# Decoder layer on one core: routing and experts in the first program, and the normaliser's magnitude and square on ScalarE

## The chip, the core and the metric

The kernel runs on one core of a Trainium2 chip. Its time is the device time of one execution in microseconds. Three executions took 796.13, 796.8 and 797.87 us, median 796.8. A profiled execution took 796.79 us. Its trace is read below; times in it count from the start of its span, which is 795.0 us long.

## The reference

A batch of 8 sequences of 256 tokens with 256 features goes through three blocks in fp32, each behind a layer norm and with a residual: gated linear attention with 16 heads; an mLSTM with 8 heads of 32; and a mixture of 8 experts, of which each token takes two.

```python
# mLSTM, per head; k_hop from a gathered table of 2017 rows
C = (qk + k_hop) * D                                  # D = exp(log_D - max_log_D)
normalizer = jnp.maximum(jnp.abs(jnp.sum(C, -1, keepdims=True)), jnp.exp(-max_log_D))
h = (C / (normalizer + 1e-6)) @ vh
hn = (h - mean(h)) / jnp.sqrt(var(h) + 1e-5)          # then weight, bias, residual
# experts
top_w, top_idx = jax.lax.top_k(logits, 2)             # then softmax over the two
for e in range(8):
    h = gelu(layernorm(x, e) @ w1[e] + b1[e]) @ w2[e] + b2[e]
    out = out + combine[..., e:e + 1] * h
```

## The kernel before

The kernel is written engine by engine: each of the five engines has its own list of instructions, and semaphores with written waits set their order. It has two programs (two `nc.Block()`), one behind the other.

The first block has three stages. The token stage (`tokens_*`) does layer norm, linear attention and the gates, batch by batch. The hop stage gathers 257 x 128 rows of the table on GpSimd's queue, turns them on TensorE, multiplies them with the queries and leaves the result in `KH`. The linear-memory stage (`mlstm_*`, lines 1104 to 1546; the mLSTM) goes over 16 units, two for each of the 8 batches. For unit `u` TensorE makes the scores (`score`), VectorE adds the hop term (`add`, lines 1429 and 1432) and multiplies with the decay (`weigh`, line 1438), for which GpSimd masks (`mask`, line 1172) and ScalarE exponentiates (`decay`, lines 1345 and 1346) a tile. TensorE multiplies with the values (`values`). The values have a column of ones, so the sum of C comes out beside h as column `DX` of the same product.

When both units of a batch are done, ScalarE copies the product from PSUM (`evict`, line 1354) and squares it (line 1358). VectorE's `spread` (lines 1440 to 1450) makes the normaliser out of column `DX` in three chained instructions on 128x16: magnitude, maximum with `EX` (with 1e-6), square times 1e-5. Then it reduces the squares to the variance (line 1448) and adds both (line 1450). The centred h needs no division by the normaliser: it scales the variance instead. ScalarE takes the inverse root (`inv_std`), VectorE multiplies (`scale`, line 1457), and GpSimd applies the weight and adds the residual (`residual`, lines 1179 and 1182). `EX` holds the exponential of the maximum; VectorE adds 1e-6 to it once (line 1500).

In the same functions, behind the last unit, stands the tail: for each batch mean and variance of the row (lines 1470 and 1477), the normalised rows (`hidden_rows`, line 1483), their turning on TensorE (line 1266), router logits (line 1277), VectorE's `add_bias` (line 1489), and a store of the rows to DRAM (`store_rows`, line 1368, the last one at line 1417) on ScalarE's queue. SyncE loads the experts' weights in `mlstm_sync` while the memory stage runs (`load_w1`, line 1098; `load_w2`, line 1101), waits for the last batch's results and clears the semaphores of the list `done_with` (`retire`). These are all that are made while `stage[0]` is `early`. The block ends at line 1547's statement, and `early.close()` frees them, so that later ones can take their numbers.

The second block is routing and experts. VectorE picks the two experts of each token and counts, TensorE makes prefix sums (lines 1868 and 1869) and, behind nine filler multiplications that the profile shows as 18 (line 1865), sorts the tokens into tiles by one-hot matrices (line 1877) that VectorE makes (`one_hot`, line 2018, and `planes`, lines 2023 to 2027). VectorE waits for the stored rows (`z_st`) ahead of `planes`, and reads the sorted result at line 2042. Then all engines loop over 39 tiles of 128 tokens: GpSimd fetches the rows (line 1831) and scatters the results with an addition (line 1851), TensorE multiplies with both weights (lines 1897 and 1906). SyncE starts this block with `prime`, 20 increments of the loop's counters, and stores the residual `X` to the output (line 1817).

## Time and profile before

| | |
|---|---|
| median of three runs | 796.8 us |
| profiled execution | 796.79 us |
| its span | 795.0 us |
| TensorE matmul busy | 731.5 us, 92% |
| VectorE busy | 408.4 us, 51% |
| ScalarE busy | 351.9 us, 44% |
| GpSimd busy | 432.1 us, 54% |
| mean granted TensorE clock | 0.974 of full speed |

The share of busy time is a mean over stages. The stages are, roughly: tokens to 200 us, hops to 355, linear memory to 444, its tail to 463, routing to 491, experts to the end. PE is TensorE, PEld its weight loads, DVE VectorE, ACT ScalarE, POOL GpSimd, SP SyncE; SPq and ACTq are their DMA queues. "L1489" is line 1489 of the kernel. `G`, `U`, `E`, `QT` and `PET` are large buffers in SBUF out of which many small tensors are cut, `ps` is PSUM.

### The profile page before, as it was taken

To read this page: it belongs to the slowest core of one execution; us is meant where nothing else is said; L and a number is where in the kernel's file an instruction comes from. 1 tells how busy PE (TensorE), PEld (TensorE's weight loads), DVE (VectorE), ACT (ScalarE), POOL (GpSimd) and SP (SyncE) were. 2 spreads that over 40 slices of the span, in tenths; PEclk is the share of its full clock that TensorE was granted. 3 is DMA by queue.
4 is the path that set the end of the run, shared out by engine and by line. 5 is a ranking of instruction groups with operands and counts; after the bars stand their busy time and mean duration, and the time that the engine had idled before them with its cause. 6 is when DMAs were issued, how large, how long until landed. Compare 5 with 4: busy or idle time off the path is not lost. (4 is left out here: it accounts for less than half of the span.)

```text
span 795.0 us, 17125 instructions
## 1 busy us (share of the span) xinstructions
PE 731.5 (92%) x5866; PEld 657.2 (83%) x5867; DVE 408.4 (51%) x982; ACT 351.9 (44%) x899; POOL 432.1 (54%) x504
## 2 busy tenths in 40 slices
PE   7899999889999999778788859999999999999992
PEld 5677777679999999777787646999999999999991
DVE  2467777756655344228999956233333333333320
ACT  1434434346665444246867411443444344434430
POOL 6567777767777777753655201244444444454432
PEclk8999999999999999899999979999999999999997
DMA  9334444432333634726777990222222122212221
GB/s 290 100 115 131 140 129 132 130 120 87 99 100 104 211 104 115 223 70 186 224 201 212 329 320 14 75 39 35 38 33 40 34 38 33 40 33 40 33 34 13
DMA packets 75813, 88.30 MB, mean 111 GB/s; under 512 B 11952, under 2 KB 66032, under 8 KB 75632
## 3 DMA queue, kind: packets, MB, share of 16 engines
q0 software_dynamic: 19824, 43.93, 22.1%
q1 hardware_dynamic: 52256, 40.12, 17.2%
q10 hardware_dynamic: 3680, 3.54, 1.3%
q8 instruction: 34, 0.56, 0.3%
q14 instruction: 19, 0.16, 0.1%
HBM read 75.83 MB, written 11.73 MB: 110 GB/s over the span
## 5 line engine op out<-in xcount | busy, mean ns | idle before, releaser
L330 POOL DMA_INDIRECT G<-in_rpe,hopi x193 | 188.6, 977 | 63.4 <-issue 53.0
L1949 ACT ACTIVATE G<-ps,U 128x128 f32<-128x128 f32 x312 | 84.7, 382 | 161.5 <-PE ps L1897 161.5
L1897 PEld LDWEIGHTS ps<-G,QT 128*128 128x128 f32 x1248 | 145.2, 192 | 1.9
L1897 PE MATMUL ps<-G,QT 128*128 128x128 f32 x1248 | 145.5, 275 | 0.0
L1906 PE MATMUL ps<-G 128*128 x624 | 142.0, 381 | 1.3 <-DVE G L2093 1.3
L1906 PEld LDWEIGHTS ps<-G 128*128 128x128 f32 x624 | 115.5, 190 | 16.3 <-issue 1.7
L1601 PE MATMUL ps<-U,PET 128*128 128x128 f32 (+3 forms) x768 | 100.3, 274 | 0.0
L1601 PEld LDWEIGHTS ps<-U,PET 128*128 128x128 f32 x768 | 94.0, 193 | 0.1
L976 DVE COPY PET<-ps 128x512 f32<-128x512 f32 x64 | 44.2, 690 | 89.3 <-PE ps L1028 87.6
L1851 POOL DMA_INDIRECT out<-G,slots x39 | 67.1, 1721 | 22.7 <-issue 22.7
L1643 ACT ACTIVATE PET<-ps 128x512 f32<-128x512 f32 (+1 forms) x63 | 37.4, 594 | 88.4 <-PE ps L1028 84.9
L1831 POOL DMA_INDIRECT G<-hidden_rows,slots x39 | 39.8, 1021 | 58.1 <-DVE U L2045 37.8
L1028 PE MATMUL ps<-cst,G 128*128 128x128 f32 x386 | 60.0, 279 | 7.3 <-DMA G<-in_rpe,hopi 7.3
L1856 POOL TENSOR_TENSOR U<-cst 128x1 f32<-128x1 f32 x39 | 7.3, 188 | 89.3 <-DMA out<-G,slots 89.3
L2063 DVE TENSOR_SCALAR G<-ps,U 128x128 f32<-128x128 f32 x78 | 28.4, 405 | 52.5 <-PE ps L1886 52.5
L1028 PEld LDWEIGHTS ps<-cst,G 128*128 128x128 f32 x386 | 46.8, 149 | 8.0 <-DMA G<-in_rpe,hopi 8.0
L675 ACT ACTIVATE U<-ps 128x512 f32<-128x512 f32 (+2 forms) x56 | 28.6, 511 | 53.1 <-PE ps L476 27.5
L1934 ACT ACTIVATE QT<-U 128x1024 f32 x39 | 43.1, 1107 | 18.5 <-DVE U L2045 18.5
L1250 PE MATMUL ps<-PET,G 128*128 128x99 f32 x256 | 41.0, 283 | 6.1 <-DVE G L1438 5.1
L330 POOL DMA_INDIRECT U<-in_rpe,hopi x38 | 37.3, 981 | 15.9 <-issue 9.1
L2051 DVE TENSOR_SCALAR QT<-U 128x1024 f32 x39 | 27.1, 695 | 35.6 <-issue 35.6
L807 DVE TENSOR_TENSOR U<-ps,cst 128x1024 f32<-128x1024 f32 x32 | 38.3, 1218 | 12.4 <-PE ps L550 8.1
(240 smaller groups left out, 1225.7 us busy)
## 6 DMA issues: line engine op xcount, KB each, us to landing
G<-run_max SPq DMA_DIRECT2D x16, 512.0 KB, 7.1
U<-in_w SPq DMA_DIRECT2D x16, 512.0 KB, 7.2
G<-in_w SPq DMA_DIRECT2D x8, 1024.0 KB, 10.3
G<-in_rpe,hopi POOLq DMA_INDIRECT x193, 2.9
U<-in_ctx SPq DMA_DIRECT2D x8, 256.0 KB, 2.8
tokens_kept<-X SPq DMA_DIRECT2D x8, 256.0 KB, 2.3
X<-tokens_kept SPq DMA_DIRECT2D x1, 2048.0 KB, 9.5
hidden_rows<-QT ACTq DMA_DIRECT2D x8, 256.0 KB, 7.3
```

The costliest lines, as they stand in the source:

```text
L330: pool.indirect_dma_start(out=dst, out_offset=None, in_=rpe_d, in_offset=bass.IndirectOffsetOnAxis(ap=hopi[:, n:n + 1], axis=0)) \
L807: nc.vector.tensor_tensor(am[n % 2], s, tri.unsqueeze(1).unsqueeze(1).to_broadcast([P, 4, 2, P]), ALU.mult).then_inc(am_r, 1)
L976: copy(PET[:, q % NPT, 0:w], bank(turn_bank(q), 512)[:, 0:w]).then_inc(pet_r[q % 2], 1)
L1028: mm = pe.transpose(o[:, n % 2, j, :], src[:, j * P:(j + 1) * P], ident)
L1250: pe.matmul(o, Dm[u % ND][:, hh, c * P:(c + 1) * P], v[0], start=True, stop=(c == 0), skip_group_check=True)
L1601: mm = pe.matmul(o, pet[:, n % 2, j, :], rhs, start=True, stop=True, skip_group_check=True)
L1831: pool.indirect_dma_start(out=z_in[u], out_offset=None, in_=z_dram, in_offset=bass.IndirectOffsetOnAxis(ap=tokg[:, u:u + 1], axis=0)) \
L1851: pool.indirect_dma_start(out=out_d, out_offset=bass.IndirectOffsetOnAxis(ap=tok[:, u:u + 1], axis=0), in_=ysb[u], in_offset=None, bounds_ ...
L1897: mm = pe.matmul(bank(1 + 2 * u + c // 4, 4, P)[:, c % 4], w1c[u][:, k, c], hT[u][:, k, :], start=(k == 0), stop=(k == KC - 1))
L1906: mm = pe.matmul(bank(7, 2, D)[:, u], gel[u][:, c, :], w2s[:, one(e), c, :].rearrange("p o n -> p (o n)"), start=(c == 0), stop=(c == NI - 1))
L1934: nc.scalar.activation(w1c[u][:, 1], w1_of(e, 1), ACT.Copy) \
L1949: ins = nc.scalar.activation(gel[u][:, c, :], bank(1 + 2 * u + c // 4, 4, P)[:, c % 4], ACT.Gelu, bias=b1c[u][:, c:c + 1])
```

## The change

Two things are changed.

One program: the second block's five functions become `experts_sync`, `experts_gpsimd`, `experts_tensor`, `experts_scalar` and `experts_vector`, made by `experts()` ahead of the one block that is left, and each engine calls its own behind its `mlstm_*`. Their bodies are as they were, but for a wait of VectorE for its own last `add_bias` at the start, a wait of SyncE for the stored rows ahead of the store of `X`, and `prime`, which moves. Only the semaphores of the token stage (33 by the code) are `early` now; `retire` clears them in `mlstm_sync`, behind the third load of second-layer weights, then `prime` and a new semaphore `fresh` follow. GpSimd waits for `fresh` ahead of its last residual, TensorE, ScalarE and VectorE in the tail.

The normaliser: ScalarE's `evict` takes the magnitude of column `DX` straight from PSUM into `nrm` ahead of its copy, and squares `nrm` behind the other square, with 1e-6 and the root of 1e-5 as bias and scale. `EX` is squared in the same way once, in place of line 1500. VectorE is left with the maximum of the two squares, which gives the same value since both are positive.

```diff
-        stage = [early]
+        stage = [late]
@@ ahead of mv_r, ..., sm_r
+        stage[0] = early
@@ behind them
+        stage[0] = late
@@ mlstm_sync
             for e in range(3):
                 sp.wait_ge(pv_full, tiles_dead(e))
                 load_w2(sp, e)
+
+            retire(sp)
+            prime(sp, counters, counters)
+            sp.sem_inc(fresh, 1)
             for e in range(NUNIT // 2 - 2, E):
...
             sp.wait_ge(lg_cp, B)
-            retire(sp)
@@ mlstm_gpsimd
             residual(B - 2)
+            pool.wait_ge(fresh, 1)
             residual(B - 1)
@@ mlstm_tensor
             logits(2)
+            pe.wait_ge(fresh, 1)
             keep_going(1)
@@ mlstm_scalar, evict
+                nc.scalar.activation(nrm[b % 2], o.rearrange("p c (h d) -> p c h d", d=NVX)[:, :, :, DX], ACT.Abs).then_inc(nrm_r, 1)
                 nc.scalar.activation(hs[b % 2].rearrange("p c h d -> p c (h d)"), o, ACT.Copy).then_inc(hs_r, 1)
                 act.wait_ge(hs_r, b + 1)
                 if b >= 1:
                     act.wait_ge(var_r, b)
-                nc.scalar.activation(sq, hs[b % 2][:, :, :, 0:DX], ACT.Square).then_inc(sq_r, 1)
+                nc.scalar.activation(sq, hs[b % 2][:, :, :, 0:DX], ACT.Square)
+                act.wait_ge(nrm_r, b + 1)
+                squared(nrm[b % 2]).then_inc(nsq_r, 1)
+
+            def squared(a):
+
+                return nc.scalar.activation(a, a, ACT.Square, scale=LN_EPS ** 0.5, bias=eps_ap[:, 2:3])
@@
             if at == "turned":
+                act.wait_ge(ex_r, 1)
+                squared(EX[:, :, :]).then_inc(ex_r, 1)
                 keys(0)
@@ the tail
+            act.wait_ge(fresh, 1)
             for b in range(3, B - 1):
                 row_inv_std(b)
@@ mlstm_vector, spread
-                dve.wait_ge(hs_r, b + 1)
-                link(nc.vector.scalar_tensor_tensor(nrm[u], hs[u][:, :, :, DX], -1.0, hs[u][:, :, :, DX], ALU.mult, ALU.max))
-                link(nc.vector.scalar_tensor_tensor(nrm[u], nrm[u], MLSTM_EPS, exv, ALU.add, ALU.max))
-                link(nc.vector.scalar_tensor_tensor(nrm[u], nrm[u], LN_EPS, nrm[u], ALU.mult, ALU.mult))
-                dve.wait_ge(sq_r, b + 1)
+                dve.wait_ge(nsq_r, b + 1)
+                nc.vector.tensor_tensor(nrm[u], nrm[u], exv, ALU.max)
@@
-            dve.wait_ge(ex_r, 1)
-            link(nc.vector.tensor_scalar(EX[:, :, :], EX[:, :, :], MLSTM_EPS, None, ALU.add))
+            dve.wait_ge(ex_r, 2)
+            dve.wait_ge(kh_cp[1], NGRP // 2)
             dve.wait_ge(kh_cp[0], NGRP // 2 + 1)
@@
             add_bias(2)
+            dve.wait_ge(fresh, 1)
             moments(7)
@@ the second block, each engine's function
+            def experts_sync(sp):
+                sp.wait_ge(z_st, 16 * (B + 1))
                 sp.dma_start(out_d[0:B * S].rearrange("(t p) d -> p t d", p=P), X[:, :, :]).then_inc(f_st, 16)
...
+            def experts_vector(dve):
+                dve.wait_ge(lg_cp, B)
                 link = Chain(dve, f_ch)
@@ the first block, each engine
                 mlstm_vector(dve)
+                experts_vector(dve)
```

## Rows read from the trace of the kernel before

**Rows 1.** Busy us (instructions) by stretch: PE, PEld, DVE, ACT, POOL; clock, DMA share, GB/s

```profile
375.00:395.00 20.00, 16.95 (x178) 15.85 (x179) 19.62 (x22) 14.54 (x40) 12.73 (x12) 1.00 0.77 217
...
490.30:788.00 297.70, 288.87 (x1962) 268.52 (x1960) 98.81 (x314) 121.83 (x351) 127.61 (x191) 0.99 0.22 38
```

**Rows 2.** Chain that ended last, in order of time: start us, us, what

```profile
473.27 9.78 PE ps L1865 x18
483.05 7.15 PE ps L1877 x64
```

**Rows 3.** Timeline at the seam: start us, us, engine, line, instruction [idle before <-releaser]

```profile
461.26 1.34 PE L1277 MATMUL ps<-U,G 128*128 128x128 f32 x10
...
462.64 0.17 DVE L1489 TENSOR_TENSOR U<-ps,PET 128x16 f32<-128x16 f32 x1 [0.78 <-PE ps L1277]
467.80 0.29 DVE L1967 TENSOR_REDUCE PET<-U 128x16 f32<-128x128 f32 x1 [4.99 <-PEq L1547]
...
469.00 0.38 SPq L1817 DMA_DIRECT2D out<-X  x1
```

**Rows 4.** Busy time by stretch, TensorE's slow stretch after the seam, columns as rows 1

```profile
472.05:477.27 5.22, 5.22 (x9) 2.70 (x10) 4.21 (x19) 1.50 (x2) 0.00 (x0) 0.50 0.87 292
```

**Rows 5.** Memory stage: timeline of PE; then busy us by stretch, PE alone

```profile
398.04 0.71 PE L1232 MATMUL ps<-QT,G 32*128 32x256 f32 x8 [2.18 <-DVE G L1432]
```
```profile
398.77:402.18 3.41, 3.41 (x23) 0.50 0.87 238
```

**Rows 6.** Timelines of POOL, ACT and DVE, a batch's normaliser under the masks

```profile
370.14 1.22 POOL L1172 TENSOR_SCALAR_AFFINE_SELECT G<-G 128x512 f32<-128x512 f32 x2 [5.14 <-DMA G<-run_max]
...
380.13 3.91 POOL L1172 TENSOR_SCALAR_AFFINE_SELECT G<-G 128x512 f32<-128x512 f32 x4
...
381.00 0.59 ACT L1354 ACTIVATE G<-ps 128x528 f32<-128x528 f32 x1
381.62 0.63 ACT L1358 ACTIVATE G<-G 128x512 f32<-128x512 f32 x1
381.71 0.61 DVE L1444 SCALAR_TENSOR_TENSOR G<-G 128x16 f32<-128x16 f32 x1
...
383.52 0.69 DVE L1448 TENSOR_REDUCE G<-G 128x16 f32<-128x512 f32 x1
...
384.24 0.17 DVE L1450 SCALAR_TENSOR_TENSOR G<-G 128x16 f32<-128x16 f32 x1
```

**Rows 7.** Timeline of DVE, the normaliser of the first and the last batch

```profile
371.70 0.19 DVE L1444 SCALAR_TENSOR_TENSOR G<-G 128x16 f32<-128x16 f32 x1 [1.81 <-ACT G L1354]
...
448.64 0.18 DVE L1444 SCALAR_TENSOR_TENSOR G<-G 128x16 f32<-128x16 f32 x1
```

**Rows 8.** Timeline of ACT, a small copy from PSUM and its follower

```profile
356.54 0.26 ACT L1643 ACTIVATE U<-ps 128x64 f32<-128x64 f32 x1
356.64 0.59 ACT L1337 ACTIVATE PET<-ps 128x512 f32<-128x512 f32 x1
```

**Rows 9.** Timeline of DVE, last one-hot planes and look at the sorted tokens

```profile
484.35 2.35 DVE L2018 TENSOR_TENSOR QT<-cst,PET 128x1024 f32<-128x1024 f32 x2
...
490.29 0.26 DVE L2042 TENSOR_SCALAR U<-ps,cst 128x39 f32<-128x39 f32 x1 [2.47 <-PE ps L1877]
```

**Rows 10.** The last store of hidden rows (timeline, DMA issues) and VectorE behind its wait

```profile
461.20 1.20 ACTq L1417 DMA_DIRECT2D hidden_rows<-QT  x1
```
```profile
hidden_rows<-QT ACTq DMA_DIRECT2D x1, 128.0 KB, 7.9
```
```profile
477.52 0.81 DVE L2023 TENSOR_TENSOR G<-cst,PET 128x624 f32<-128x624 f32 x1
```

**Rows 11.** Timeline of SyncE's queue, first-layer loads of the last two experts

```profile
432.10 2.96 SPq L1098 DMA_DIRECT2D U<-in_w  x1
...
441.89 1.25 SPq L1098 DMA_DIRECT2D U<-in_w  x2
```

**Rows 12.** Timeline of POOL in the expert loop

```profile
516.48 0.19 POOL L1850 TENSOR_TENSOR U<-cst 128x1 f32<-128x1 f32 x1 [0.47 <-DVE G L2093]
```

494 lines of the change are left out of this document (247 added, 247 removed).

## The prediction, made before the change was run

> **What bounds the kernel now.** I read the views in this order: busy time by stretch, to find the engine that each stage waits for; the chain of waits, to see what lies between the stages; the timeline over the seam between the two programs; and the timelines of the normaliser on ScalarE, VectorE and GpSimd. Two stages matter. In the linear-memory stage VectorE is the busiest engine: 19.62 of the 20 us from 375 to 395, TensorE 16.95, ScalarE 14.54. In the expert loop it is TensorE, busy 288.87 of 297.70 us [rows 1]. So an instruction that VectorE loses in the first stage can count in full, and nothing that the change does can shorten the second: it can only start it sooner. Between them lies a stretch where little runs. TensorE's last logits end at 462.60 (461.26 + 1.34) and VectorE's last bias addition at 462.81; the first instruction of the routing starts on VectorE at 467.80, after 4.99 us put down to line 1547, which is the block and no tensor [rows 3]. From there the chain runs over VectorE's picks to TensorE's prefix sums at 472.05 [rows 4], the filler multiplications (9.78 us) and the 64 multiplications that sort the tokens (7.15 us) [rows 2], and from their end to the loop. Everything from 467.80 on hangs on that start.
>
> **The seam.** Before, SyncE waits for the last bias addition and only then clears the first stage's semaphores (80 by the code) and lets the block end; all engines meet, and enter the next one. The second block's first work on SyncE is 20 increments, and its first transfer goes out at 469.00, 1.20 us after VectorE has started: 60 ns for each of the 20 [rows 3]. At that price the 80 clears are 4.8 of the 4.99 us, and the meeting some 0.2. The estimate of the split isn't needed: both parts leave VectorE's path. What stands in their place is VectorE's wait for its own last bias addition. Such a wait between two of its small instructions is some hundredths of a microsecond, so the first pick starts between 462.84 and 463.0. I take 4.9 us.
>
> **What is moved onto SyncE's queue.** The clears that are left (33) and the 20 increments, with one more for the new signal, now stand behind the third load of the second-layer weights and ahead of the first-layer loads, of which one went out at 432.10 and the last two at 441.89, when an addition of VectorE let them [rows 11]. 54 instructions at 60 ns are 3.2 us. Meanwhile the queue has three loads of 1 MB to work off, so the transfer engines don't run dry; the loads of 441.89 wait for VectorE anyway, which covers the delay. I cost it at nothing. Without that cover the stream of weights ends 3.2 us later, and the hidden rows with it. Four engines wait for the new signal, each ahead of the work on its last batches; GpSimd is the first there, behind its last but one residual and so behind VectorE's 16th unit, later than 441.89, and the signal is given at about 435.3.
>
> **What is late next.** Three things could take the place of the seam. First the hidden rows: the last store is issued at 461.20 and lands 7.9 us later, at 469.1. VectorE waits for it ahead of the instruction that started at 477.52 [rows 10]; with the change it gets there at about 471.7, so 2.6 us are spare. This store shares the engines with weight loads, so it hardly moves when the stage before is shortened. The store of the residual moves from 469.00 to just after 469.1, and its first user is the first scatter, after the sort. Second, the sorting multiplications need VectorE's last one-hot planes, which ended at 486.70. The last 16 of 64 multiplications need them and take 7.15/4 = 1.8 us, so they could have ended at 488.5; they ended at about 490.2 [rows 2, 9]. TensorE is later than VectorE by 1.7 us, and both move with the seam. Third, TensorE's clock.
>
> **TensorE's clock.** After the seam TensorE runs from 472.05 to 477.27 at a granted clock of 0.50, the 1.2 GHz level [rows 4]; at 2.4 GHz the same work takes half, so this stretch costs 2.6 us. TensorE had been idle for 9.45 us. With the change it is idle from 462.6 to about 467.1, 4.5 us. In the linear-memory stage it idled for 2.18 us up to 398.04, and from 398.77 on the clock was at 0.50 for 3.41 us [rows 5]. A pause of 4.5 us is twice that, so I expect it to fall again. The slow work after it may last 3.4 us, as there, or as much longer than 5.2 as that is shorter, 7.0: 0.9 us less to 0.9 us more. I take nothing. If it doesn't fall, TensorE gains 2.6 us, of which VectorE's planes let 1.7 through.
>
> **The normaliser.** Of eight batches, each loses on VectorE three chained instructions on 128x16 and gets one maximum. ScalarE gets a magnitude ahead of its copy and a square behind the other square, and VectorE waits for the last of these. Under GpSimd's masks (380.13 to 384.04) the three cost 1.81 us, from 381.71 to the reduction at 383.52; this is so in four of the eight batches [rows 6]. The undisturbed price of one of them is 0.18 us [rows 7]. A magnitude on 128x16 isn't in the trace: its nearest row is a ScalarE copy of 128x64 from the same memory, 0.26 us, whose follower started 0.10 us after it [rows 8]. So the magnitude delays the copy by 0.10 to 0.26 us, and the small square, 0.2 us with 0.1 of it under the end of the large one, adds 0.1 to 0.26. ScalarE's large square ended at 382.25; the small one ends between 382.45 and 382.77, nearer the first, since such instructions overlap: I take 382.5. VectorE starts its maximum then and pays between 0.2 and 0.6 us, the two prices seen [rows 6, 7]. The reduction starts between 382.7 and 383.4, against 383.52. The last small instruction of the batch (384.24) then comes at 383.4 to 384.1, when the masks may still run, and would pay up to 0.4 us more. But the masks end sooner too: they take 0.98 us each under VectorE's instructions and 0.61 alone (two in 1.22) [rows 6], and VectorE now leaves GpSimd the pause from 381.8 to 382.5. So a batch gains between -0.1 and 0.7; I take 0.4, and 1.6 for the four.
> The other way round it goes where VectorE already waits for ScalarE. In the first batch it waited 1.81 us for the copy and started at 371.70; in the last one it started at 448.64; each time three instructions at 0.18 us with small gaps, 0.65 us in all, stood ahead of the reduction [rows 7]. There the new wait ends 0.9 us after the old start (the large square with 0.63 us, and 0.25 for the two small ones), the maximum adds 0.1 before the reduction may start beside its end, and 0.65 are saved: 0.35 later each, 0.7 together, 1.1 if nothing overlaps. The two remaining batches lie between; I take them at nothing, within 0.2 each. The addition of a constant to EX, which VectorE is rid of, stood ahead of its wait for the very copy of rows 8, so it gives nothing; ScalarE's square in its place comes before its part of that stage, in a pause for TensorE's last products. No table is loaded for it: the square is already used there. Sum for this part: 1.6 - 0.7 = 0.9 us, bounds -1.9 (four at -0.1, 1.1 and 0.4) and 2.6 (four at 0.7, -0.6 and 0.4).
>
> **Sum.** The profiled execution took 796.79 us (span 795.0), and the median of the runs is 796.8, so nothing has to be shifted. 4.9 + 0.9 = 5.8 us off: 791.0 us.
>
> **The rivals.**
> (a) VectorE waits for ScalarE in every batch, and what it saves is lost. In the mild form its maximum meets the masks and costs 0.61 us instead of 0.2 in four batches [rows 6]: 1.6 us less, 792.6. In the strong form both ScalarE instructions also run unoverlapped, -1.9 in place of 0.9: 793.8. For it speaks that one of the three takes 0.61 under the masks and 0.18 without [rows 6, 7]; against it, that VectorE's new pause lets the masks finish sooner. Chances 0.13 and 0.07.
> The Trainium skill (SBUF — State Buffer, Who interferes with whom) says that a VectorE instruction with two inputs in SBUF blocks against a GpSimd instruction that reads SBUF, and the maximum is one with two such inputs. By that rule alone the mild form is the forecast; the trace agrees with the rule for the three that go.
> (b) The clock stays up: 1.7 us more gain, 789.3 us. For it, the pause is halved; against it, the clock's fall in [rows 5]. Chance 0.10.
> (c) Slower than before. In the expert loop GpSimd is nearly as late as TensorE: it idles only 0.47 us ahead of its use of a tile's result [rows 12]. The loops are entered in another phase between GpSimd, VectorE and TensorE. If in that phase the scatter lands 0.7 us later behind its issue, GpSimd's cycle is 0.2 us longer than TensorE's, over 39 tiles 7.8 us: 796.8 - 5.8 + 7.8 = 798.8. It decides once the 0.47 us are used up. Against it: the loop's waits pull every phase to the same one within a few tiles, and its code is unchanged. Chance 0.05.
> (d) The change doesn't do what it says: VectorE's pause stays because something else than the block fills it, code fetched for the routing or the hidden rows landing 3.2 us late behind SyncE's clears. The latter alone would put the rows at 472.3 against a need at 471.7, 0.6 us. A full replacement of the 4.9 us leaves the normaliser's 0.9: 795.9, no change. Chance 0.06.
>
> **How the numbers follow.** The forecast with the scatter of its terms (seam 4.8 to 5.0, normaliser 0 to 2, clock -0.9 to 0.9) has 0.59; (a) 0.20, (b) 0.10, (c) 0.05, (d) 0.06. The range goes from (b) with a good normaliser, 788.4, to near (a), 793.5. This measurement can tell about 0.2%, 1.6 us, from no change. Faster by more than that: the forecast, (a) and (b), 0.89. Within it: (d) and a remnant, 0.06. Slower: (c), 0.05.
>
> **What would show it.** The pause of VectorE behind the last bias addition should be under 0.3 us, and TensorE's pause near 4.5. From VectorE's first pick to its look at the sorted tokens (467.80 to 490.29) it should take 22.5 us as before, less or more by what the clock does, and from there to the end of the span 304.7 us, as now. The small square should end 0.1 to 0.5 us behind the large one, and VectorE should show a wait for ScalarE ahead of the maximum in all eight batches. The eight batches should take about a microsecond less than now. The prediction is wrong if VectorE's pause keeps over 1 us, if it waits at the planes for the hidden rows, if the eight batches take longer than before, or if the loop's period moves.

## The result, and the profile after

The changed kernel takes 795.63 us (median of 22 runs, 792.09 to 798.17); the kernel before took 798.03 us in the 22 runs beside it. The ratio is 0.9966, with a 95% interval of 0.9953 to 0.9978. So it is faster, by 2.7 us by this ratio and 2.4 by the medians, where 5.8 were forecast, and the 795.63 lie above the range of 788.4 to 793.5. The profiled execution took 794.85 us with a span of 793.0, against 796.79 and 795.0 before.

What was forecast for the time up to the expert loop came true in the main. The timeline over the former seam (start us, us, engine, line, instruction, idle time before it) shows VectorE's last bias addition and its first pick, and TensorE's prefix sums:

```profile
462.07 0.17 DVE L1505 TENSOR_TENSOR U<-ps,PET 128x16 f32<-128x16 f32 x1 [0.78 <-PE ps L1285]
462.27 0.29 DVE L1775 TENSOR_REDUCE PET<-U 128x16 f32<-128x128 f32 x1
...
466.53 0.80 PE L1677 MATMUL ps<-PET,cst 128*128 128x128 f32 x2 [4.50 <-DVE PET L1784]
```

The first pick starts 0.20 us behind the start of the last addition, where it started 5.16 us behind it [rows 3]. TensorE's pause is 4.50 us, as worked out. VectorE's look at the sorted tokens, which was at 490.29 [rows 9], is 6.18 us earlier, 0.57 of them gained up to the last addition, 4.96 in the seam and 0.65 from the pick to the look:

```profile
484.11 0.26 DVE L1850 TENSOR_SCALAR U<-ps,cst 128x39 f32<-128x39 f32 x1 [1.80 <-PE ps L1686]
```

From there to the end of the span the profile before has 304.7 us, and this one 308.9. That is where the gain went: 4.2 us, in two parts. The last store of results is issued at 780.79 instead of 784.26, 3.47 us earlier; so 2.7 us are lost in the 39 tiles. And behind it the end of the span comes 12.2 us later, not 10.7. The last pieces of the chain that ended last (start us, us, what), of the kernel before and then of the changed one:

```profile
784.26 1.55 POOL out L1851
785.81 2.27 issue
788.08 0.23 POOLq L1813
```
```profile
780.79 1.55 POOL out L1661
782.35 2.27 issue
784.61 0.23 POOLq L1909
```

In the loop, TensorE's product of a tile stands 0.22 us behind the transposes in the profile before. Here it is further behind in 13 of 37 tiles, seldom in two that are neighbours, mostly by up to 0.16 us, and in one it is 0.77 us behind. That is the worst place, PE alone:

```profile
677.55 3.73 PE L1706 MATMUL ps<-G,QT 128*128 128x128 f32 x32
681.13 0.38 PE L1695 MATMUL ps<-cst,G 128*128 128x128 f32 x2
681.90 3.72 PE L1715 MATMUL ps<-G 128*128 x16 [0.39 <-issue]
```

Over 32 tiles the mean period of VectorE's additions of the second bias (L2090 before, L1898 after) is 7.265 us before and 7.339 after. "issue" means that the profile shows nothing for which the engine waited, and that is the question of the experiments.

### The profile page after: what moved, and what is told of

The parts are those of the page before. It is cut to its first block, busy times and chain, and to the rows that moved or that the text cites. A ratio compares the mean times of both kernels' runs of the same rounds, so it can differ in the third digit from the quotient of the medians.

```text
span 793.0 us, 17064 instructions
## 1 busy us (share of the span) xinstructions
PE 732.1 (92%) x5866; PEld 656.5 (83%) x5867; DVE 405.2 (51%) x966; ACT 354.6 (45%) x916; POOL 434.5 (55%) x504
## 4 chain that ended last, share of the span: by engine, by line
PE 38%; issue 26%; POOL 19%; DVE 7%; ACT 5%; DMA 3%; POOLq 1%; DVEq 0%; ACTq 0%
PE ps L1965 10%; POOL out L1661 8%; POOL G L1641 5%; PE ps L1031 5%; PE ps L485 4%; POOL G L332 3%; DMA G<-in_rpe,hopi 2%; PE ps L552 2%; PE ps L526 2%; PE ps L478 2%; ACT G L1354 2%; PE ps L450 1%; PE ps L576 1%; PE ps L1674 1%; ACT G L1355 1%
## 5 line engine op out<-in xcount | busy, mean ns | idle before, releaser
L979 DVE COPY PET<-ps 128x512 f32<-128x512 f32 x64 | 44.2, 690 | 89.3 <-PE ps L1031 87.6
L1641 POOL DMA_INDIRECT G<-hidden_rows,slots x39 | 39.9, 1024 | 53.7 <-DVE U L1853 32.1
L1666 POOL TENSOR_TENSOR U<-cst 128x1 f32<-128x1 f32 x39 | 7.4, 189 | 90.2 <-DMA out<-G,slots 90.2
```

Of the source, the lines that this page charges most:

```text
L979: copy(PET[:, q % NPT, 0:w], bank(turn_bank(q), 512)[:, 0:w]).then_inc(pet_r[q % 2], 1)
L1641: pool.indirect_dma_start(out=z_in[u], out_offset=None, in_=z_dram, in_offset=bass.IndirectOffsetOnAxis(ap=tokg[:, u:u + 1], axis=0)) \
```

## The experiments

The time of a kernel is a median of its runs; "before" is the kernel before in the runs beside them. The three columns that follow are from the profile of each kernel: the look at the sorted tokens, from there to the issue of the last store, and from that to the end of the span.

| kernel | time, us | before, us | look at | look to last store | last store to end |
|---|---|---|---|---|---|
| before | | 798.0 | 490.3 | 294.0 | 10.7 |
| after (the change) | 795.6 | 798.0 | 484.1 | 296.7 | 12.2 |
| seam_only | 796.4 | 797.9 | 484.5 | 297.0 | 12.1 |
| norm_only | 798.7 | 797.9 | 489.5 | 296.4 | 10.7 |
| drain | 791.7 | 797.9 | 486.0 | 294.3 | 10.7 |
| hoist | 792.7 | 797.9 | 484.4 | 293.3 | 12.1 |
| norm_hoist | 796.2 | 798.2 | 491.5 | 293.0 | 10.6 |
| before_hoist | 797.6 | 798.1 | 491.9 | 293.3 | 10.7 |
| drain_hoist | 790.4 | 798.2 | 486.0 | 293.2 | 10.8 |
| drain_mid | 794.1 | 798.2 | 482.4 | 295.5 | 12.0 |
| drain_tail | 788.5 | 798.2 | 484.4 | 296.8 | 4.4 |
| tail4_put | 783.7 | 798.1 | 484.8 | 292.4 | 4.6 |
| pad | 798.5 | 798.1 | 490.7 | 295.4 | 10.6 |
| pad_wide | 858.2 | 858.7 | 555.9 | 294.8 | 10.6 |
| pads3 | 862.2 | 858.3 | 553.1 | 296.7 | 10.5 |
| shift | 849.3 | 853.5 | 539.9 | 295.0 | 12.2 |
| drain_shift | 846.7 | 853.5 | 539.9 | 294.4 | 10.8 |
| before_shift | 853.6 | 853.5 | 548.1 | 294.2 | 10.6 |

The column "look at" has the noise of the hop stage in it: the last copy of that stage starts anywhere from 352.1 to 356.1 us, whatever the kernel. The last five rows ran on chips on which that stage ends between 407 and 416 us for every kernel; they are compared with the kernel before on the same chip.

### Each part alone

seam_only is the changed kernel with the old normaliser (its three instructions back on VectorE, no magnitude and no second square on ScalarE).

> The merged program with the old normaliser. The seam's own theory of the prediction: 4.9 us off, so the look at the sorted tokens comes at about 485.3 instead of 490.29. What the trace after the change added: from that look to the end of the span it took 308.9 us instead of 304.7, of which 1.3 us lie behind the last scatter's landing (GpSimd's drain took 8.17 us, against 6.68) and the rest in the 39 tiles. If that loss belongs to the merging, this kernel has it whole: loop and end 308 to 309 us, and only some 0.7 to 1.5 us are left of the 4.9. If it belongs to the normaliser's change (through the time at which the loop is entered) or to chance, loop and end take 304.7 us here and the kernel is 4.9 us faster than before.

796.37 us (12 runs), ratio 0.9975 (0.9957 to 0.9993), 1.5 us faster. The seam is gone (first pick 0.21 us behind the last addition), and the loss is there whole: 297.0 us and 12.1 us, as in the changed kernel. Both losses belong to the merging.

norm_only is the kernel before with the new normaliser.

> Two programs as before, with the magnitude and the squares on ScalarE. By the prediction's sum 0.9 us faster than before, by its bounds 2.6 faster to 1.9 slower; the tail of the memory stage should start 0.9 us earlier (443.3 against 444.19, as in the trace after the whole change). Loop and end take 304.7 us and the last drain 6.7 us if both losses belong to the merging. If the loop's loss comes from being entered at another time, it may show here too, with up to 3 us.

798.73 us (12 runs), ratio 1.0013 (0.9997 to 1.0029): no gain. The look comes 0.8 us earlier (it is taken apart below). The end keeps its 10.7 us. But the loop takes 2.4 us more, though nothing in it is changed. VectorE's additions of the second bias show a rhythm: one comes 7.14 us behind the one before it and the next mostly 7.4 to 7.6. TensorE's own steps don't have it (7.25 to 7.4 us for most, twice 7.67), but in nearly every second tile its product is late, with 0.22 us from transposes to product and then 0.37:

```profile
628.35 0.38 PE L1894 MATMUL ps<-cst,G 128*128 128x128 f32 x2
628.57 3.62 PE L1914 MATMUL ps<-G 128*128 x16
632.02 3.73 PE L1905 MATMUL ps<-G,QT 128*128 128x128 f32 x32
635.59 0.38 PE L1894 MATMUL ps<-cst,G 128*128 128x128 f32 x2
635.96 3.72 PE L1914 MATMUL ps<-G 128*128 x16
```

So there are two ways in which this loop loses time, and the second needs no merging.

### What the block's end did for GpSimd

drain puts one instruction into the changed kernel, at a place where GpSimd is idle:

```diff
             def experts_gpsimd(pool):
...
+                nc.gpsimd.drain()
                 pool.wait_ge(z_st, 16 * (B + 1))
```

> The changed kernel with one more instruction: GpSimd drains its pipeline at the start of the experts' part, where it has nothing to do until the rows are stored. Theory 1: GpSimd carries a state of its 257 gathers into the loop, which the drain at the first block's end used to clear; this state makes the issue of its transfers later by 0.07 us a tile and the last drain longer. Then with the drain the time from the end of the last store to the fetch falls back from 0.82 to 0.75 us, TensorE's period to 7.27 us, the last drain to 6.7 us, and the kernel gains 4.2 us: about 791. Theory 2: the longer last drain and the loop's loss have to do with where the code lies or with the phase in which the loop is entered: no change, loop and end stay at 308.9 us. The last drain alone may return to 6.7 (1.5 us) while the loop keeps its loss; then the two losses have different causes.

791.66 us (6 runs, 791.39 to 793.27), ratio 0.9919 (0.9900 to 0.9938). What theory 1 gives is there, nearly to the number: the last drain takes 6.69 us, look to last store 294.3 us, mean period 7.277. The effect on single tiles can be read off GpSimd's timeline: from the start of the small instruction behind a store's landing (L1856, L1666, L1667) to the next fetch (L1831, L1641). Before, it takes 0.76 us:

```profile
630.56 0.19 POOL L1856 TENSOR_TENSOR U<-cst 128x1 f32<-128x1 f32 x1 [2.36 <-DMA out<-G,slots]
...
631.32 1.02 POOL L1831 DMA_INDIRECT G<-hidden_rows,slots  x1 [0.42 <-issue]
```

In the changed kernel it takes 0.83 us, and some stores are issued late too (0.96 us of "issue" in front of one, where 0.58 is usual):

```profile
621.32 1.60 POOL L1661 DMA_INDIRECT out<-G,slots  x1 [0.96 <-issue]
625.25 0.19 POOL L1666 TENSOR_TENSOR U<-cst 128x1 f32<-128x1 f32 x1 [2.34 <-DMA out<-G,slots]
...
626.08 1.03 POOL L1641 DMA_INDIRECT G<-hidden_rows,slots  x1 [0.47 <-issue]
```

With the drain it is back at 0.75 us:

```profile
641.04 0.18 POOL L1667 TENSOR_TENSOR U<-cst 128x1 f32<-128x1 f32 x1 [2.35 <-DMA out<-G,slots]
...
641.79 1.02 POOL L1641 DMA_INDIRECT G<-hidden_rows,slots  x1 [0.42 <-issue]
```

That looked like one cause. It is two, as the next runs show.

drain_mid puts the same instruction into the token stage instead, at its fifth batch, behind 69 of the 257 gathers.

> The changed kernel with GpSimd's drain in the middle of the token stage, behind about a quarter of the 257 gathers, and none later until the end. It shows whether the state that the drain clears grows with the transfers made since, or comes at once. If it grows, some 190 gathers and 78 transfers stand behind this drain, and the last drain takes between 6.7 and 8.2 us, about 7.7; the fetch's delay may fall back to 0.75 us in part of the loop. If any gathers at all bring it, the last drain stays at 8.17 us and the delay at 0.82 us, and the time at 795.6.

794.12 us (10 runs), ratio 0.9951 (0.9931 to 0.9970). The last drain took 8.16 us, behind 266 transfers, as behind 335. But the fetch was not late in the way of the changed kernel: the time from landing to fetch, tile by tile, has two patterns laid over each other. In the changed kernel every second tile (no back edge between) takes 0.82 to 0.83 us (the first 1.06), and in drain_mid 0.76. In both alike, the stores of tiles 16 and 23 are issued 0.36 us late, from tile 25 on every store but the last is some 0.07 late, and in the last tiles the fetch is 0.07 later once more.

shift, drain_shift and before_shift were made for that. shift has an instruction that clears nothing where drain has the drain:

```diff
             def experts_gpsimd(pool):
...
+                nc.gpsimd.tensor_tensor(pool_pad[:, 6:7], ones[:, 0:1], ones[:, 1:2], ALU.mult)
                 pool.wait_ge(z_st, 16 * (B + 1))
```

> The changed kernel with one small instruction of GpSimd (0.19 us, in its idle time) at the place where the other kernel has the drain: it moves the code of GpSimd's loop on by one instruction and clears nothing. A closer reading of the records has made this needed: with a drain in the token stage the last drain stays at 8.16 us and the stores stay late (0.91 us from VectorE's result to the store, against 0.86), yet the fetch is issued 0.76 us behind the landing up to the 24th tile, as in the kernel before, and only then later. So the 0.07 us of the fetch may have to do with where the loop's code lies, and the stores and the last drain with what the gathers leave. Theory A (place of the code): fetch 0.76 us, stores 0.91, last drain 8.17, look to last store 295.5 us, in all about 794.4. Theory B (all of it is left by the gathers): fetch 0.83 us, 296.7 us, 795.6 in all.

> The changed kernel with the drain and, behind it, the same small instruction: GpSimd's loop lies two instructions further on, and the state is cleared. By theory B nothing changes against the drain alone: 791.7, fetch 0.76 us. By theory A the delay of the fetch may be another one than 0.76 us (0.83 or more) while the stores stay at 0.86 us and the last drain at 6.69: 791.7 to 793.

> The kernel before with the same small instruction of GpSimd at the start of its second block. By theory B no change: fetch 0.754 us, 798.0. By theory A the fetch may come later, 0.8 us or more, and the loop take up to 1.5 us longer.

shift: 849.31 us (12 runs) where before takes 853.5, ratio 0.9954 (0.9938 to 0.9970). The fetch is issued after 0.76 us, though nothing is drained; the stores of tiles 16 and 23 and those from 25 on are as late as in the changed kernel, the last drain takes 8.17 us, look to last store 295.0 us. That is theory A. drain_shift: 846.71 us (6 runs), 0.9924 (0.9901 to 0.9948), with a fetch at 0.75 us, no late store, a last drain of 6.69 and 294.4 us; one more step of the code changes nothing. These two ran side by side, and differ in the drain alone. before_shift: 853.60 us (12 runs), 0.9989 (0.9968 to 1.0010), everything as before. So of the 4.2 us that the changed kernel loses:

- 1.5 us are the longer last drain (12.2 against 10.7),
- about 0.7 us are the late stores (295.0 against 294.3 and 294.4 with the drain); these and the first item are gone once GpSimd has drained behind its gathers,
- about 1.7 us are the fetch's 0.07 us (296.7 against 295.0), gone in every kernel with one or two more instructions of GpSimd ahead of the loop. All kernels whose loop lies where the change puts it have it (after, seam_only, hoist), and no other one. That it is the place of the code is the reading that fits; the profile doesn't show how. The size is less sure than the effect: drain_mid has the same issue times as shift and takes 295.5 us, which would leave 1.2, and in the times the gain of shift over the changed kernel (ratios 0.9954 and 0.9966) is within their intervals.

The rest is what kernels without late issues vary by (294.0 in before, 294.2 in before_shift, 294.3 and 294.4 with the drain).

### How the loop loses it

hoist lets TensorE's queue read the expert's number of a tile (an address for the product) before the transposes:

```diff
                 def step(n, u, i):
                     if live(n + 1):
                         up(n + 1, 1 - u, i + u)
+                    e = pe.value_load(tile_e[0:1, one(n)], min_val=0, max_val=E - 1)
                     if live(n + 2):
                         turn_z(n + 2, u, i + 1)
-                    down(n, u, i)
+                    down(n, u, i, e)
```

> The changed kernel, in which TensorE's queue reads the expert's number of a tile ahead of the transposes instead of behind them. In the trace after the change the loop's loss shows as a gap of 0.22 to 0.77 us between the transposes and the second product in every second tile: the rows that GpSimd fetched land late, the queue passes their wait late, and then needs some 0.95 us (of them 0.5 for reading the number) before it can issue the product. If that is how the loss reaches TensorE, the gap is 0.22 us everywhere, the period 7.25 us, and loop and end take about 2.5 us less than the 308.9 (the last drain stays at 8.2). If TensorE waits for the rows themselves, the gap goes to the front of the transposes and the period stays at 7.33 us: no gain.

792.71 us (6 runs), ratio 0.9933 (0.9913 to 0.9953). The gap is 0.22 us everywhere, the period 7.245 us, look to last store 293.3 us. GpSimd's fetch is as late as in the changed kernel (0.833 us in the mean) and the last drain takes 8.17 us. So the lateness is still there, and no longer reaches TensorE. That holds for both causes at once. From the look to the end it is 3.6 us shorter than in the changed kernel, more than the 2.5 expected, since the loop of the kernel before wasn't at TensorE's pace either (7.265 us).

norm_hoist and before_hoist make the same edit in norm_only and in the kernel before.

> Two programs, the new normaliser, and the expert's number read ahead of the transposes. With the normaliser alone the look at the sorted tokens came 0.87 us earlier than before (489.42), as the prediction's sum has it, but the loop fell into another rhythm: TensorE's steps alternated between 7.14 and about 7.5 us, and from the look to the last scatter's issue it took 296.4 us instead of 294.0, with GpSimd's issue times unchanged. Theory: that rhythm lives on the chain store, landing, fetch, landing, transposes, address, product, which for two tiles is as long as two of TensorE's steps (14.5 us); with 0.5 us taken out of it TensorE sets the pace alone, 7.25 us in each step, and look to last scatter takes 293.3 us as in the kernel with the number read early: 795.0 to 795.5 in all. Rival: the loss of the normaliser's kernel comes from something else (VectorE's or ScalarE's part of the loop); then the rhythm of 7.14 and 7.5 stays, and the time stays at 798.7.

796.16 us (12 runs), ratio 0.9967 (0.9953 to 0.9981). The loss is gone: TensorE's products start 7.25 us apart in every tile, the period is 7.245, look to last store 293.0 us. The rhythm itself isn't gone. VectorE's additions still come 7.14 and 7.35 us apart, here 7.35:

```profile
603.64 0.42 DVE L2098 TENSOR_TENSOR G<-ps,G 128x256 f32<-128x256 f32 x1 [0.69 <-PE ps L1913]
...
610.99 0.42 DVE L2098 TENSOR_TENSOR G<-ps,G 128x256 f32<-128x256 f32 x1 [1.16 <-PE ps L1913]
```

Their products start at 599.85 and 607.09, so the addition stands 3.79 us behind one and 3.90 behind the other; in before_hoist it is 3.79 in every tile. So VectorE's part of every second tile is 0.11 us later in both kernels with the new normaliser and two programs. In norm_only that would come on top of a chain without slack, and here the early number gives the chain room; but no run takes the 0.11 us away by itself. The rival had this right, that VectorE's part differs, but not that the loss would stay. The time is 0.7 us more than the upper end of what was expected, and the hop stage in its profile ended 2.8 us later than before.

> The kernel before with only the expert's number read ahead of the transposes. It is the partner of the kernel that has the new normaliser and the same early number (796.16): if the normaliser alone is worth the 0.6 to 0.9 us that the times at which the stages end show, this one takes 796.8 to 797.1; if the normaliser is worth nothing, or its loss was real and not one of the loop's rhythm, it takes 796.2 or less. Its loop should have TensorE's period at 7.245 us instead of 7.265, 0.7 us in all.

797.56 us (12 runs), ratio 0.9993 (0.9976 to 1.0011). With the loop at TensorE's pace in both, the normaliser alone is worth 797.56 - 796.16 = 1.4 us; the scatter of these runs is some 2 us, so this agrees with 0.9 and doesn't prove it.

Three kernels turn it round: in the kernel before, further small instructions of GpSimd stand ahead of each fetch (one of 128x1 in pad, one of 128x32 in pad_wide, three of 128x1 in pads3), behind the one that is there:

```diff
                         nc.gpsimd.tensor_tensor(pool_pad[:, 4 + u:5 + u], ones[:, 0:1], ones[:, 1:2], ALU.mult)
+                        for v in range(3):
+                            nc.gpsimd.tensor_tensor(pool_wide[:, 2 * v + u:2 * v + u + 1], ones[:, 0:1], ones[:, 1:2], ALU.mult)
```

> The kernel before with one more small instruction of GpSimd (0.19 us) ahead of each fetch. Theory: the chain from the product's result over the store's landing, the fetch, its landing, the transposes and the address is as long as two of TensorE's steps, 14.5 us, though GpSimd itself idles some 0.5 us a tile ahead of its use of the result. Each fetch comes 0.15 to 0.2 us later, the chain of two tiles takes 14.65 to 14.7, so the period goes from 7.265 to 7.32 to 7.35, which is 2 to 3 us over the loop: 800 to 801. By the prediction's reading (the 0.47 us of idle time are GpSimd's slack) nothing changes: 797.9.

> The kernel before with one more multiplication of GpSimd, 128x32, ahead of each fetch. The smaller one made the fetch only 0.034 us later (0.788 us behind the landing instead of 0.754) and the mean period went from 7.265 to 7.299, too little to tell anything in the time (798.5 against 798.1). Theory: the chain of two tiles through the fetch has no slack against two of TensorE's steps of 7.245 us, so a delay of d per fetch lengthens a tile by half of d: for d of 0.15 to 0.25 us the period goes to 7.34 to 7.39, and the kernel takes 2.5 to 5 us longer, 800.5 to 803. The reading of the prediction, that GpSimd's 0.47 us of idle time ahead of its use of a result are its slack: no change, 798.1, since the delay is smaller.

Both missed their size: the fetch came only 0.034 us later, since the added instruction runs in time that GpSimd had spent ahead of the fetch anyway: the 0.42 to 0.48 us of "issue" there fall to 0.31 to 0.37. The periods were 7.299 and 7.287 us, the ratios 1.0004 and 0.9993, no difference.

> The kernel before with three more small instructions of GpSimd ahead of each fetch. One of them, small or wide, made the fetch only 0.034 us later, so neither run told anything; three should make it 0.2 to 0.5 us later. Theory: the chain of two tiles through the fetch is as long as two of TensorE's steps (14.5 us), so a delay of d lengthens a tile by half of d: 0.1 to 0.25 us, 4 to 10 us over 39 tiles, 802 to 808 where before takes 798. The prediction's reading: GpSimd idles 0.47 us ahead of its use of a result, and a smaller delay than that is absorbed: 798.

862.23 us (12 runs), ratio 1.0034 (1.0014 to 1.0054), 3 us slower by the ratio and 3.9 by the medians. Its row shows 0.92 us in place of 0.76:

```profile
694.49 0.19 POOL L1859 TENSOR_TENSOR U<-cst 128x1 f32<-128x1 f32 x1 [2.35 <-DMA out<-G,slots]
...
695.41 1.02 POOL L1832 DMA_INDIRECT G<-hidden_rows,slots  x1 [0.16 <-issue]
```

In the tiles behind the loop's back edge the delay is 0.10, so 0.135 in the mean, less than the 0.2 to 0.5 that I had expected. The period is 7.347 us, 0.082 more than before, where half of the delay would be 0.07; look to last store takes 2.7 us more. It isn't the rhythm of norm_only: the short steps of VectorE's additions are 7.25 us here, not 7.14. A delay well below 0.47 us isn't absorbed: GpSimd's idle time is no slack.

### Versions that beat both

drain_hoist has both edits.

> The changed kernel with both: GpSimd's drain ahead of the experts and the expert's number read ahead of the transposes. The early number alone gave a period of 7.245 us and 293.25 us from look to last scatter; the drain alone took 1.4 us off the end. If the two losses are as separate as that, their gains add at the end only: about 1.0 us less than the drain alone (791.7), so 790.5 to 791.0.

790.36 us (6 runs, 789.65 to 791.84), ratio 0.9890 (0.9867 to 0.9914), 0.1 us below what was expected.

drain_tail adds a second drain of GpSimd, in the unrolled tail of the loop:

```diff
                                             compute_op=ALU.add).then_inc(scat, 16)
+                    if isinstance(n, int) and n == NT - 3:
+                        nc.gpsimd.drain()
 
                     pool.wait_ge(scat, 16 * (n + 1))
```

> As the former, with one more drain of GpSimd in the unrolled last tiles: behind the issue of the third scatter from the end, ahead of the wait for its landing. Theory 1 says that the length of a drain follows from the transfers issued since the one before: 6.69 us behind 78, 8.17 behind 335, 0.17 at the start of the kernel behind none. If it is nearly proportional from nothing, the last one, behind 2 transfers, takes under 2 us, while the added one hides in GpSimd's idle time of some 5 us a tile there: 785 to 787 us. If a drain has a fixed part of some 6 us as soon as any transfer was made, the last one stays at 6 to 6.7 us and the added one delays the last two scatters by up to 2 us: 790 to 793 us.

788.45 us (4 runs), ratio 0.9877 (0.9845 to 0.9909), between the two theories. The drain at the end takes 0.47 us behind 2 transfers, so its length depends on what was issued since the last one, though not in proportion and not on the count alone (0.17 us behind none, 6.69 behind 78, 8.17 behind 335, but 6.53 behind the 257 gathers at the former block's end, the last residual's 1.27 us included). But the added one, which holds GpSimd for 6.3 us behind the store's issue, delayed the last store by 3.6 us: the next two stores wait for GpSimd, and VectorE in turn waits for a store's landing before it touches the next result.

tail4_put moves the drain one tile forward, for which GpSimd's last five tiles are unrolled instead of three, and loosens that wait of VectorE in the last tiles from the store before (n - 1) to the one before that (n - 2), whose buffers are the ones that are used again.

> The changed kernel with the drain ahead of the experts, the early number, and a last drain hidden better than with three tiles to go: GpSimd's last five tiles are unrolled instead of three, the added drain stands behind the issue of the fourth store from the end, and VectorE waits in the last tiles for the store before the last one instead of the last one. Three tiles ahead the drain (6.5 us) delayed the last store by 3.6 us, and the drain at the end fell from 6.69 to 0.47 us. With one more tile to catch up, and VectorE not held, the last store should be no more than 1 us late: 785 to 786.5 us. If the delay goes on through the tiles all the same, 788.

783.65 us (5 runs, 782.80 to 784.84), ratio 0.9816 (0.9797 to 0.9835): 14.4 us faster than the kernel before and 12 faster than the changed one, better than expected. Which of the two edits gave how much was not tried apart. GpSimd's timeline from the drain (6.29 us of "issue" ahead of the row of 766.37) to the end:

```profile
758.19 1.88 POOL L1662 DMA_INDIRECT out<-G,slots  x1 [0.57 <-issue]
766.37 0.19 POOL L1669 TENSOR_TENSOR U<-cst 128x1 f32<-128x1 f32 x1 [6.29 <-issue]
766.52 0.19 POOL L1661 TENSOR_TENSOR U<-cst 128x1 f32<-128x1 f32 x1
767.19 1.57 POOL L1662 DMA_INDIRECT out<-G,slots  x1 [0.49 <-issue]
...
777.23 1.55 POOL L1662 DMA_INDIRECT out<-G,slots  x1 [0.53 <-issue]
781.07 0.19 POOL L1669 TENSOR_TENSOR U<-cst 128x1 f32<-128x1 f32 x1 [2.29 <-DMA out<-G,slots]
```

The fourth store from the end stands at 758.19, and the last is issued at 777.23, 0.9 us earlier behind the look than in drain_hoist. The span ends at 781.8, 0.7 us behind the last landing.

## Why the prediction was wrong, point by point

**The seam: right.** 4.9 us were forecast. In seam_only the first pick follows the last addition after 0.21 us, and the block's 4.99 us are gone. The rival (d), that something else fills the pause, is out.

**SyncE's moved instructions, the hidden rows, the planes: right.** VectorE doesn't wait ahead of `planes` (its first one starts at 472.00 behind its own chain). TensorE is still later than VectorE at the sort, 1.80 us in the row of 484.11.

**The clock: right in kind.** It fell again behind the pause of 4.50 us, and the range of 0.9 less to 0.9 more held. Stretch, then busy us and count of PE, PEld, DVE, ACT and POOL, granted clock, DMA share, GB/s:

```profile
466.46:469.87 3.41, 3.34 (x7) 2.03 (x8) 2.51 (x14) 1.50 (x2) 0.00 (x0) 0.51 0.73 257
```

3.41 us at 1.2 GHz instead of 5.22 [rows 4], and 21.8 us from the pick to the look where I had 22.5. But norm_only, in which TensorE's pause is 9.46 us as before, needs 21.8 us as well. Over all 18 profiles it takes 21.6 to 22.8 us, with either normaliser and with or without the seam. So this 0.65 us can't be put down to the change. The rival (b) is out: the clock didn't stay up.

**The normaliser: right in the sum, and mostly in its terms.** One batch under GpSimd's masks, ScalarE and then VectorE, which now waits for ScalarE in all eight batches:

```profile
382.81 0.17 ACT L1363 ACTIVATE G<-ps 128x16 f32<-128x16 f32 x1
382.88 0.60 ACT L1364 ACTIVATE G<-ps 128x528 f32<-128x528 f32 x1
383.51 0.63 ACT L1368 ACTIVATE G<-G 128x512 f32<-128x512 f32 x1
384.05 0.29 ACT L1374 ACTIVATE G<-G,eps 128x16 f32<-128x16 f32 x1
```
```profile
384.37 0.35 DVE L1463 TENSOR_TENSOR G<-G,EX 128x16 f32<-128x16 f32 x1 [0.77 <-ACT G L1374]
```

The magnitude delays the copy by 0.07 us (0.10 to 0.26 forecast), the small square ends 0.20 us behind the large one (0.1 to 0.5), and the maximum costs 0.35 us under the masks and 0.19 elsewhere (0.2 to 0.6). From one batch's variance to the next, norm_only has, in us of VectorE's records, 10.39, 10.74, 12.74, 10.40, 10.73, 10.10 and 10.35 where before has 11.09, 11.08, 12.56, 11.07, 11.09, 9.92 and 10.05. So four steps gain 0.7, 0.3, 0.7 and 0.4 (0.4 each forecast), the last batch loses 0.3 (0.35 forecast), the first, seen from the hop stage's end, 0.5 (0.35), and the two that I had put at nothing lose 0.2 each. In sum 0.9 us from the hop stage's end to the last variance, as forecast. In norm_only that stage ended 0.8 us later than before, and the clock gave 0.65 us (above), hence its look only 0.8 us earlier; my expectation for norm_hoist took those 0.8 for the normaliser's by mistake. From the hop stage's last copy to the tail's first mean the nine kernels with the new normaliser take 89.3 to 90.2 us and the four with the old one on the same chips 90.8 to 91.4; 0.3 of that go back in the last batch, which lies in the tail. The changed kernel itself got less: 95.5 us from the hop stage's last copy to the last variance against 96.0, because its first variance came 21.0 us behind that copy, where the others on these chips need 19.0 to 19.6, and not all of that was made up; hoist and drain_tail have it too, and why isn't shown. So 0.5 us of the forecast 0.9 was left at its last variance. Rival (a) is out up to the loop. The masks didn't finish sooner, though: four of them take 3.92 us as before [rows 6], so the reason that I gave for the gain in the tail of a batch was wrong. The Trainium skill's rule on a VectorE instruction with two inputs in SBUF (SBUF — State Buffer, Who interferes with whom) agrees in kind: the maximum takes nearly twice as long under the masks. It costs far less than the 0.61 us of the instruction that went.

**That the loop, with its code unchanged, takes 304.7 us to the end: wrong, and this is the step that failed.** The sum put this term at nothing. It stands in the part on what bounds the kernel ("can only start it sooner"), and in the words against rival (c). Two things were wrong in it.

First, the end of a block isn't only clears and a meeting, and the same source isn't the same program. GpSimd's drain stood in the block's end, hidden under the tail, and I gave it no line because it cost nothing there. What it did for the work behind it was the thing to cost: without it stores in the loop are issued late and the last drain takes 1.5 us longer (the runs with the drain put back show both gone). And merging moved the loop's code, and one small instruction (shift) undoes what seems to come of that. I had a reason against neither; I hadn't asked.

Second, the slack. I read GpSimd's idle 0.47 us ahead of its use of a result [rows 12] as the distance to TensorE's pace. But that wait is for VectorE's result, and so for TensorE itself. The chain that competes with TensorE runs through the next fetch: VectorE's addition, the store's issue, its landing, the fetch, its landing, the transposes, the address, the product, and VectorE's addition two tiles on. Typical pieces of the kernel before are 1.8 us from the addition to the store's issue, 3.85 to the landing, 1.1 to the fetch, 2.8 to the rows (the median of the DMA issues), 0.95 for the queue from the rows to the product, and 3.9 from there to the addition: 14.4 us against two of TensorE's steps, 14.5. So 0.1 us was spare, and not in every tile, since the landings vary by 0.2 us. The place of 681.13 in the changed kernel, link by link:

```profile
670.47 0.42 DVE L1898 TENSOR_TENSOR G<-ps,G 128x256 f32<-128x256 f32 x1 [0.73 <-PE ps L1715]
```
```profile
672.61 1.93 POOL L1661 DMA_INDIRECT out<-G,slots  x1 [0.93 <-issue]
```
```profile
676.95 0.19 POOL L1666 TENSOR_TENSOR U<-cst 128x1 f32<-128x1 f32 x1 [2.41 <-DMA out<-G,slots]
677.38 0.19 POOL L1656 TENSOR_TENSOR U<-cst 128x1 f32<-128x1 f32 x1 [0.25 <-issue]
678.06 1.02 POOL L1641 DMA_INDIRECT G<-hidden_rows,slots  x1 [0.48 <-issue]
```
```profile
G<-hidden_rows,slots POOLq DMA_INDIRECT x39, 2.8
```
```profile
685.78 0.42 DVE L1898 TENSOR_TENSOR G<-ps,G 128x256 f32<-128x256 f32 x1 [1.36 <-PE ps L1715]
```

This is tile 23, one of the two late stores. The store is issued 2.14 us behind the addition instead of 1.8, takes 1.93 us itself where 1.59 is usual and lands 4.34 us after its issue began instead of 3.85, the fetch comes at 678.06 and its rows near 680.9, TensorE's queue passes the wait and reads the address at 681.05, and the product starts at 681.90. From addition to addition it is 15.3 us. The waits that I trusted to pull every phase to the same one don't do it: norm_only stayed in its rhythm of 7.14 and 7.5 us to the end of the loop, and norm_hoist in one of 7.14 and 7.35.

**Rival (c) named the cycle, but not what lengthened it, and mis-sized it.** It had GpSimd's scatter landing 0.7 us later behind its issue, a cycle longer by 0.2 us and 7.8 us over the loop, with a chance of 0.05. The landings are as before (4.01 us behind the start of the issue in the mean, 4.03 now); it is the issues that are late. The cycle of a tile grew by 0.074 us and the loop by 2.7, together with 1.5 at the end: 796.8 - 6.2 + 2.7 + 1.5 = 794.8, the time of the profiled execution. The chance was too low because the slack was read from the wrong wait.

**What stays open.** What the state is that GpSimd's drain clears, why a drain takes 8.17 us behind 266 transfers as behind 335 and only 6.53 behind 257 gathers, and why the lateness shows at the same tiles. How the place of GpSimd's code makes a fetch late in one of two tiles: that it is the place is inferred from which kernels have it. What makes VectorE's addition 0.11 us later in every second tile of norm_only and norm_hoist; it is so from the first tile on (first step 6.89 us in both), and the changed kernel with the same normaliser doesn't have it. Whether drain_mid's hop stage ended early (352.1 us) because of the drain in the token stage or by chance.

## What to carry to other kernels

Slack of an engine is not its idle time but the length of the cycle through it, added up link by link (queue and address instructions too) and set against the pace of the engine that bounds; where the two are within a few hundredths, an unchanged loop can change its time with an edit ahead of it. When a block boundary is removed, list what each engine does there, hidden work included, and ask what it leaves behind for the next stage; here one drain put back into idle time, with the step by which it moved the code, was worth 4 us. And a fix that works is no proof of its reason: only the same edit without its supposed effect (an instruction that drains nothing) told the two causes apart. What no engine computes behind the last transfer is part of the time as well: a drain that was due at the end was cheap to take earlier, once there were tiles enough behind it to catch up.

## What the runs showed of the hardware

- GpSimd's drain takes 0.17 us behind no transfer, 0.47 behind 2 (drain_tail), 0.55 behind 3 (tail4_put), 6.69 behind 78 and 8.17 behind 266 or 335 indirect transfers, with all of them landed. It is not the count alone: behind the 257 gathers it takes 6.53, of which 1.27 lie beside the last residual. The same 335 transfers with a drain between cost 6.69 at the end.
- Without a drain behind the gathers, GpSimd issues two stores of the loop 0.36 us late (tiles 16 and 23) and all but the last from tile 25 on some 0.07 us late, in every kernel of that kind, whether there was a drain among the gathers or not. The Trainium skill (DMA: Bandwidth & Descriptors, SWDGE vs HWDGE vs iDMA) says that software on GpSimd writes the descriptors of its transfers into rings in SBUF; a state of these rings would fit, and no run here shows it.
- One instruction more ahead of GpSimd's loop (drain, shift, drain_mid) or none decides whether a fetch in every second tile is issued 0.83 or 0.76 us behind a landing.
- A small instruction of GpSimd ahead of an indirect transfer may cost nearly nothing: 0.034 us for one of 0.19 (pad), 0.10 to 0.17 for three (pads3).
- TensorE's queue needs some 0.95 us from the wait ahead of the transposes to the next product when it reads an address between them. By this sum it is hidden as long as the rows land a microsecond before the product is due; with the address read ahead of the transposes (hoist) it never shows.
- On some chips the stages up to the end of the hop stage take 54 to 63 us longer (to 407 to 416 us instead of 353) for every version of the kernel that ran there, and the loop doesn't.
